# Cross-attention kernel: the output projection of a tile made in two halves, in two slots, and the projections dealt anew over the slots

## What is computed

```python
x = x + xattn(layernorm(x), ctx, ctx, mask, w_q, w_k, w_v, w_o)
x = x + ffn(layernorm(x), kernel, bias, a, b)

# xattn
q, k, v = query @ w_q, key @ w_k, value @ w_v          # 256 -> 16 heads x 64
scores = einsum('bhqd,bhkd->bhqk', q, k) / sqrt(64)
scores = where(mask, -inf, scores)
out = einsum('bhqk,bhkd->bhqd', softmax(scores), v)
return out @ w_o                                       # 1024 -> 256
# ffn: y = x @ int4(kernel) + bias + (x @ a) @ b
```

## Time and profile before

| | |
|---|---|
| median of 3 runs | 517.91 us (517.69, 517.91, 519.60) |
| the profiled execution | 519.61 us, its span 517.8 us |
| TensorE clock granted | 0.96 on average; 1.00 from about 80 us to 486 us |
| busy: PE / DVE / ACT / POOL | 448.1 / 412.6 / 324.6 / 393.3 us |
| batch of 16 slots, steady | 54.77 us; with h, r0, r1 57.50 us |

### The profile page before, as it was taken

How to read it: one execution, slowest core, us unless ns; L and a number is a source line. 1 busy time by engine, 2 the same in 40 slices (tenths; PEclk the granted TensorE clock), 3 DMA queues, 4 the chain that set the end, 5 groups by cost and what they waited for, 6 DMA issues and landing times.

```text
span 517.8 us, 15453 instructions
## 1 busy us (share of the span) xinstructions
PE 448.1 (87%) x5855; PEld 328.1 (63%) x5855; DVE 412.6 (80%) x1122; ACT 324.6 (63%) x837; POOL 393.3 (76%) x652
## 2 busy tenths in 40 slices
PE   3219768999999999999999999999999999888873
PEld 0116246667866686677766786668666866666652
DVE  4955756888899897978898888989897978887662
ACT  4905446577667776677667766777677766665621
POOL 3356158798978897788879888889788887899941
PEclk9658979999999999999999999999999999999898
DMA  8320139767796699679967797669868886679950
GB/s 308 120 61 11 30 58 202 130 128 152 169 175 130 128 199 154 114 122 176 173 130 137 161 167 149 132 133 192 161 122 146 141 159 128 134 128 182 165 122 26
DMA packets 218817, 71.91 MB, mean 139 GB/s; under 512 B 202785, under 2 KB 216882, under 8 KB 218738
## 3 DMA queue, kind: packets, MB, share of 16 engines
q1 hardware_dynamic: 217680, 69.25, 69.6%
q0 software_dynamic: 480, 1.31, 1.1%
q10 hardware_dynamic: 578, 0.30, 0.2%
HBM read 14.71 MB, written 4.19 MB: 37 GB/s over the span
## 4 chain that ended last, share of the span: by engine, by line
PE 45%; DVE 28%; ACT 14%; POOL 6%; issue 3%; DMA 3%; POOLq 0%; DVEq 0%; ACTq 0%
PE ps_b L874 34%; ACT arena L646 8%; DVE ps_a L764 7%; PE ps_a L939 6%; DVE arena L757 4%; DVE arena L746 2%; ACT arena L637 2%; ACT arena L625 2%; PE ps_b L982 2%; PE ps_b L958 2%; DVE arena L712 2%; DVE arena L768 1%; DVE arena L837 1%; POOL arena L564 1%; POOL arena L560 1%
## 5 line engine op out<-in xcount | busy, mean ns | idle before, releaser
L874 PE MATMUL ps_b<-arena 128*128 128x65 f16 (+3 forms) x3384 | 328.8, 250 | 10.9 <-DVE arena L837 3.4
L874 PEld LDWEIGHTS ps_b<-arena 128*128 128x128 f16 x3384 | 226.8, 98 | 90.5 <-issue 5.9
L646 ACT ACTIVATE arena<-ps_a,arena 128x160 f32<-128x160 f32 x512 | 159.5, 394 | 95.8 <-DVE arena L768 88.5
L564 POOL TENSOR_TENSOR arena<-arena 128x512 f16<-128x512 f32 x128 | 148.1, 1157 | 0.0
L560 POOL CAST arena<-arena 128x512 f16<-128x512 f32 x128 | 78.1, 610 | 64.6 <-ACT arena L646 62.8
L764 DVE TENSOR_REDUCE ps_a<-ps_a 128x4 f32<-128x640 f32 x128 | 105.3, 822 | 0.0
L939 PE MATMUL ps_a<-arena 64*128 64x160 f16 x1536 | 76.8, 233 | 16.8 <-ACT arena L646 15.0
L939 PEld LDWEIGHTS ps_a<-arena 64*128 64x128 f16 x1536 | 51.2, 95 | 41.4 <-issue 23.8
L958 PE MATMUL ps_b<-arena 128*128 128x65 f16 x512 | 71.6, 194 | 0.0
L757 DVE TENSOR_TENSOR arena<-ps_b,arena 128x512 f16<-128x512 f32 x64 | 43.5, 686 | 24.5 <-ACT arena L637 23.7
L837 DVE TENSOR_TENSOR arena<-ps_b,arena 128x256 f32<-128x256 f32 x128 | 54.3, 424 | 4.4
(11 more groups left out here) (130 smaller groups left out, 401.5 us busy)
## 6 DMA issues: line engine op xcount, KB each, us to landing
arena<-in_x_dram SPq DMA_DIRECT2D x8, 512.0 KB, 5.2
mask_u<-in_x_dram SPq DMA_DIRECT2D x32, 128.0 KB, 3.1
out_dram<-mask_u SPq DMA_DIRECT2D x32, 128.0 KB, 2.8
arena<-arena SPq DMA_TRANSPOSE x128, 3.9
arena<-arena SPq DMA_DIRECT2D x24, 65.0 KB, 2.5
arena<-in_L_xattn_w_k_dram SPq DMA_DIRECT2D x1, 1024.0 KB, 8.1
arena<-in_L_xattn_w_v_dram SPq DMA_DIRECT2D x1, 1024.0 KB, 10.1
arena<-in_L_xattn_w_q_dram SPq DMA_DIRECT2D x1, 1024.0 KB, 11.9
```

The source lines that it names most:

```text
L564: nc.gpsimd.tensor_tensor(lo_main, main, hi_main, ALU.subtract)
L646: ins = nc.scalar.activation(probs[k % 2][:, h, :], p_scores[k % 2][:, h % 2, h // 2 * WINDOW:(h // 2 + 1) * WINDOW], ACT.Exp, bias=neg_ma ...
L874: mm = nc.tensor.matmul(dst, a, c, start=(first and at == 0), stop=(last and at == n - 1))
```

## The change

`LATE` moves w from g = 1 to g = 0, where PE makes only its first four terms (`last=False`) and signals nothing; a new step, `finish_output`, adds the other four into the same bank in the slot after (g = 1), after the weighted values and ahead of that slot's projections, and signals then. `PROJ` is dealt anew: slots 1, 5, 9 and 13 now have projections, 8 and 12 have none.

```diff
-        PROJ = [["c", "x0"], [], ["x1"], ["k0", "k1"],
-                ["k2", "k3"], [], ["q0"], ["q1"],
-                ["q2", "q3"], [], ["q4"], ["q5"],
-                ["q6", "q7"], [], ["v0"], ["v1"]]
-        QUAD_ITEMS = {5: "h", 7: "r0", 11: "r1"}
-        LATE = [[("n", 3)], [("w", 2)], [("f", 3), ("o0", 1)], [("o1", 1)]]
+        PROJ = [["c"], ["x0", "x1"], ["k0"], ["k1", "k2"],
+                ["k3"], ["q0"], ["q1"], ["q2"],
+                [], ["q3"], ["q4"], ["q5"],
+                [], ["q6"], ["q7"], ["v0", "v1"]]
+        QUAD_ITEMS = {1: "h", 9: "r0", 13: "r1"}
+        LATE = [[("n", 3), ("w", 2)], [], [("f", 3), ("o0", 1)], [("o1", 1)]]
...
                 elif name == "w":
                     pe.wait_ge(item_done, items_at[s.k - 1])
-                    mm = halves(bank[:, 0:D], [(oT_hi[:, m, :], oT_lo[:, m, :], wt(3, 0)[:, m, :],
-                                                wt(3, 1)[:, m, :]) for m in range(HT)])
+                    halves(bank[:, 0:D], [(oT_hi[:, m, :], oT_lo[:, m, :], wt(3, 0)[:, m, :],
+                                           wt(3, 1)[:, m, :]) for m in range(HT // 2)], last=False)
+                    return
...
+            def finish_output(s):
+
+                bank = p_item[s.bank(len(s.proj) + len(s.late) - 1)]
+                pe.wait_ge(item_done, items_at[s.k])
+                halves(bank[:, 0:D], [(oT_hi[:, m, :], oT_lo[:, m, :], wt(3, 0)[:, m, :],
+                                       wt(3, 1)[:, m, :]) for m in range(HT // 2, HT)], first=False) \
+                    .then_inc(item_made, 1)
...
             def slot(s):
...
+                if s.g == 1 and 0 <= s.k // NG - 2 < NT:
+                    finish_output(Slot(s.k - 1))
```

## The result

The changed kernel takes 551.55 us (551.28 to 551.77, 4 runs) against 517.88 us before: ratio 1.0646, 95% interval 1.063 to 1.0662. The forecast was 552 us, with a range of 530 to 564.

A forecast was written before the change was run, and what follows sets the result against it. PE sets the pace before; after, the ring and o1's bank do. Four batches 22.4, seventh 4.8, third 3.5, first 4, tail -0.6 us: +34 on the 517.9 median, 552 us; range 530 to 564.

The forecast's parts named there:

- The ring: Path projection, ScalarE high half, VectorE low half, maxima, exponentials, scores: 3.50 us a round, 14.45 us for slots 5 to 9.
- The other tiles: Slots 9 to 13 take 15.35 us, slots 13 to 1 16.0, slots 1 to 5 14.6.
- the bank of o1: In slots 13 to 1 and 1 to 5, w's first half waits for it, until 12.3 and some 10.9 us.
- The +4 of the first batch: First batch: two more rounds of the ring, +4 us (2 to 6), an estimate.
- The end: Last batch costs 0, unchanged at 11.05 us a tile; POOL's shorter variance wait in the tail gives -0.6 us.
- What would show it: Signs in the profile after: 60 us batches, exponentials 3.50 us apart, and named waits before scores, n and L814.
- my upper bound: VectorE's wait for w delays the next division 0.25 us a tile: hidden, but 7 us in the upper bound.
- The slack of 0.3 us: Before the change, slot 8's exponentials ended at 367.02 and its scores began at 367.31; the ring cost nothing.
- rows 2: Profile rows of PE's waits before the change: about 8 us between 119 and 450 us, in three recurring places.
- Faster: Rival, 6%: the ring has unseen slack, PE stays the bound, evened slots remove waits: about 508 us.
- Half the loss: Rival, 17%: only slots 5 to 13 pay, +2.9 us a batch, +18 in all: 536 us.
- the clock is gated by how busy the engine has been of late: Skill's rule: TensorE at the forecast 88% busy should keep full clock; clock falls belong to rival "More", 6%.

The follow-up runs named there:

- Experiment 6: Changed kernel with w split into two terms in slot g = 0 and six in g = 1, instead of four and four: 561.07 us, ratio 1.0844.
- experiment 2: Changed kernel with VectorE taking w one slot later (g = 2), as before the change, and h in slot 5: 551.94 us, ratio 1.0637.
- the ring cut: Edit used in several runs: VectorE takes the maxima ahead of all low halves, not behind the first; alone on the kernel before: 508.16 us.
- experiment 1: Changed kernel with VectorE taking the maxima ahead of all low halves, instead of behind the first: 532.31 us, ratio 1.0256.
- experiment 3: Changed kernel with VectorE taking w late (g = 2), h in slot 5, and the maxima ahead of all low halves: 509.77 us, ratio 0.9838.
- Experiment 10: Kernel before the change with only VectorE's maxima moved ahead of all low halves: 508.16 us, ratio 0.9802.
- experiment 7: Kernel before with the new deal of projections, w whole behind the projections of slots g = 1, h in slot 5: 556.19 us, ratio 1.0701.
- experiment 5: Changed kernel with w's second half behind its slot's projections, VectorE taking w early (g = 1), h in slot 5: 587.0 us, ratio 1.1314.
- experiment 8: Kernel of experiment 7 with VectorE's maxima ahead of all low halves: 525.56 us, ratio 1.0131.

## Why the prediction was right

**The ring.** Its sum for slots 5 to 9 was 14.45 us; 14.27 was measured. The exponentials are 3.42 and 3.43 us apart where I took 3.50 from one pair; that is 0.15 of the 0.18.

**The other tiles.** 15.35 forecast for slots 9 to 13, 15.23 measured; 16.0 and 15.82 for slots 13 to 1; 14.6 and 14.58 for slots 1 to 5. Experiment 6 confirms which of them hang on the ring and which on the bank of o1. Beside the kernel before, the same four stretches went from 13.99 to 14.27 (slots 5 to 9), 14.52 to 15.23, 13.65 to 15.82 and 12.61 to 14.58: work moved between them too, but 4.1 of the 5.1 us that a batch grew stand in the two that hang on o1's bank, not in the 14.45 that the forecast works out with most care. A batch of 60.4 was forecast and 59.90 came: 0.5 too much, four times, with 0.5 for the third batch and 0.1 for each of the first and seventh, is 2.7 us too much; the set-up was 0.7 shorter, and the end of the kernel was forecast 1.2 too low. Together 34 against 31.9 in the spans. The medians differ by 33.7, since the profiled execution of before lay 1.7 us above its median. So that 552 came within 0.5 us is in part luck: these 1.7 us and the errors of opposite sign made it. The +4 of the first batch was an estimate, not worked out from rows, and came as 3.9.

**The end.** I had priced the last batch at nothing, since slot 11's exponentials were to come before POOL needs them. They came 0.17 us after, and a tile takes 11.26 us instead of 11.05. The mechanism was named, its size was off by 0.2 us a tile. The gain of 0.6 in the tail doesn't show.

**What would show it.** Seen as forecast: scores waiting for L646 in slots 8, 9, 12 and 13 of the sixth batch (0.20, 0.15, 0.20, 0.52 us), n waiting for L682 in slot 8 (0.34), L814 waiting 1.59. Not as forecast: n in slot 12, which does not wait; TensorE's busy share, which is 91% (54.80 of 59.90 us) instead of 88%, as its busy time grew from 53.22 us with the same matmuls; and the wait for the division, up to 0.93 us in slot 10 and 2.7 us in a batch (302.68 to 362.58), the largest of TensorE's waits. It took up TensorE's slack at another place than I had said. It did not change the sum, since the ring decided, as experiment 2 shows, in which the waits for the division fall to 1.1 us a batch and the time stays the same. With the ring cut, taking w later on VectorE is worth 22 us (experiments 1 and 3), three times the 7 us that my upper bound gave it; the waits for the division themselves are 2.2 of the 3.3 us that a batch gains by it. Had the ring been a little shorter, the forecast would have failed at this term.

**What the forecast had wrong of the kernel before.** The forecast says that the ring had slack before the change and cost nothing. Experiment 10 says that it cost 10 us. The slack of 0.3 us at one place was not slack at all sixteen: the waits of rows 2 for a bank and for the division had the same order of VectorE's queue behind them.

**The rivals.** "Faster" had evened slots remove the waits of the earlier trace rows; with the ring cut (experiment 3) the halves do run at 509.8, so the idea of the change works where VectorE's order lets it, but is then no better than the old deal with the same edit (508.2). "Half the loss" fell, as all four tiles pay. The granted clock stayed at 1.00 in the batches of the changed kernel from the second on. The Trainium skill, TensorE: Matmul & The Clock Gate (Part 1), says that the clock is gated by how busy the engine has been of late; the traces agree in part: the full clock held here at 91% busy, while in experiments 7 and 5 it fell to 0.74 and 0.77 around waits of 1.47 and 2.22 us, though not around every such wait.

## What to carry to other kernels

Before moving work between the slots of a software pipeline, write down the longest path that one slot's product takes through the in-order queues of the other engines to the next thing that the bounding engine waits for, and count how many such rounds lie between two points at which it starts afresh. An engine that is 97% busy can be within 0.3 us of being bound by such a path, and its own busy time says nothing of it. In each in-order queue put first what the bounding engine waits for soonest: here one swap on VectorE was worth 10 us in the kernel before and 11 to 42 us in the variants of the change. And count what the same swap gives the old kernel before you credit it to the new one: with it the old deal, at 508.2 us, is as fast as the best of the others.

## What I had not expected of the hardware

The clock can fall around waits of TensorE as short as 1.47 us, and what went just before does not tell whether it will. In experiment 7 the stretch from slot 5 to slot 9 is the same in the sixth and the seventh batch: 14.63 us, TensorE busy 12.96 of them, a wait of 1.47 us at the end. In the sixth, 6.62 us at a mean granted clock of 0.74 followed, between the levels of 1.2 and 2.4 GHz; in the seventh, 5.03 us at 1.00. Where the clock fell (six of 14 waits of 1.47 to 2.25 us), the wait cost twice: itself, and 1.6 to 1.7 us in the slot after it. The 14 waits of 0.64 to 0.92 us at the same places in experiment 8 were followed by no fall. What decides between the two is open.
